# The row search of a routing front in four parts, step 0's sum a group sooner, lists joined in group 13, tokens taken earlier

## The reference, cut to what matters

```python
xn = layernorm(x)                                   # x: 2 x 4096 x 256, f32
# attention with 12 sampled positions per token and head (16 heads of 16)
off = tanh(pw_w @ gelu(depthwise_conv3(q)) + pw_b) * 6
positions = clip(token + anchor + off, 0, 4095)
scores = q . sample(k, positions) / 4 - rel_scale * |positions - token|
s = (softmax(scores) . sample(v, positions)) @ wo.T + bo
# mixture of experts: 8 experts, each token uses its best 2
g = silu(sum over 2 chosen experts of gate * (silu(a) * b) @ Wl2)
out = x + s * g
```

## Time and profile before

| | us |
|---|---|
| median of 3 runs (lowest, highest) | 1420.66 (1420.04, 1420.97) |
| the profiled execution | 1421.36 |
| its span, first to last instruction | 1419.6 |
| TensorE busy in the span | 1328.6 (94%) |
| VectorE busy | 1245.7 (88%) |
| ScalarE busy | 798.7 (56%) |
| GpSimd busy | 725.6 (51%) |
| mean granted TensorE clock | 0.968 |

### The profile page before, as it was taken

One profiled execution on the slowest core, in us unless ns is written; L12 is line 12 of the kernel. 1 busy time (PEld: TensorE's weight loads), 2 busy tenths in 40 slices (PEclk: granted clock), 3 DMA queues, 4 the chain that ended last, 5 costly groups with the idle time before them and its releaser, 6 DMA issues. The chain is left out here.

```text
span 1419.6 us, 36324 instructions
## 1 busy us (share of the span) xinstructions
PE 1328.6 (94%) x13885; PEld 1063.0 (75%) x13885; DVE 1245.7 (88%) x1759; ACT 798.7 (56%) x1920; POOL 725.6 (51%) x441
## 2 busy tenths in 40 slices
PE   4998899997899999999999999999999978998987
PEld 4864455655688888888888888888888866777775
DVE  7847788788699999999999999999999999898971
ACT  2546688866655454545554454555455446676654
POOL 1001022100477888787887888886887862211031
PEclk9999999996899999999999999999999989999997
DMA  7952556964758586868777585877777569989679
GB/s 242 345 184 88 149 183 201 297 203 141 222 169 270 136 256 169 246 192 242 203 221 216 148 262 139 234 192 236 201 199 214 142 168 277 293 222 266 196 214 208
DMA packets 206905, 297.77 MB, mean 210 GB/s; under 512 B 21809, under 2 KB 164533, under 8 KB 206515
## 3 DMA queue, kind: packets, MB, share of 16 engines
q0 software_dynamic: 59968, 141.95, 38.0%
q1 hardware_dynamic: 119171, 141.43, 31.1%
q10 hardware_dynamic: 27632, 12.64, 3.5%
HBM read 186.30 MB, written 118.03 MB: 214 GB/s over the span
## 5 line engine op out<-in xcount | busy, mean ns | idle before, releaser
L1651 POOL DMA_INDIRECT moe_rows<-expert_mem,token_of x135 | 333.2, 2468 | 105.5 <-issue 71.5
L1618 POOL DMA_INDIRECT expert_mem<-xn_rows,token_of x131 | 243.7, 1860 | 48.1 <-issue 38.1
L1941 PE MATMUL pY<-expert_mem 128*128 x1080 | 253.2, 386 | 0.0
L1941 PEld LDWEIGHTS pY<-expert_mem 128*128 128x128 f32 x1080 | 199.0, 190 | 39.4 <-issue 13.6
L2139 DVE SCALAR_TENSOR_TENSOR mid<-pos_pair,mid 128x768 f32<-128x768 f32 x224 | 197.3, 950 | 0.5
L1785 ACT ACTIVATE expert_mem<-pA,b1sel 128x256 f32<-128x256 f32 (+1 forms) x300 | 110.1, 455 | 126.3 <-PE pA L1935 120.5
L1935 PE MATMUL pA<-mid,expert_mem 128*128 128x256 f32 (+1 forms) x816 | 168.3, 360 | 5.5 <-ACT mid L1757 4.9
L262 DVE SCALAR_TENSOR_TENSOR mid<-mid 128x768 f32<-128x768 f32 x192 | 169.4, 949 | 0.0
L1935 PE MATMUL pB<-mid,expert_mem 128*128 128x256 f32 (+1 forms) x816 | 166.1, 357 | 0.0
L1796 ACT ACTIVATE expert_mem<-pB,b1sel 128x256 f32<-128x256 f32 (+1 forms) x300 | 110.7, 468 | 96.1 <-PE pB L1935 96.1
L1935 PEld LDWEIGHTS pA<-mid,expert_mem 128*128 128x128 f32 x816 | 143.4, 192 | 24.2 <-ACT mid L1757 3.9
(11 more groups left out here) (282 smaller groups left out, 2408.3 us busy)
## 6 DMA issues: line engine op xcount, KB each, us to landing
expert_mem<-in_w_l POOLq DMA_DIRECT2D x51, 1024.0 KB
bandT<-in_w_l POOLq DMA_DIRECT2D x24, 1024.0 KB
band<-band_rows SPq DMA_DIRECT2D x256, 96.0 KB, 5.4
S_rows<-expert_mem SPq DMA_DIRECT2D x64, 376.0 KB, 4.7
band_rows<-wgt SPq DMA_DIRECT2D x12, 1536.0 KB
pos_pair<-pos_rows SPq DMA_DIRECT2D x28, 384.0 KB
xn_rows<-expert_mem SPq DMA_DIRECT2D x16, 512.0 KB, 5.6
v_rows<-expert_mem SPq DMA_DIRECT2D x16, 512.0 KB, 4.5
```

What stands on the lines that cost most here:

```text
L1618: nc.gpsimd.indirect_dma_start(out=xs[:, u, s], out_offset=None, in_=dram["xn"], in_offset=bass.IndirectOffsetOnAxis(ap=keep["inv"][:, 2 * ...
L1651: nc.gpsimd.indirect_dma_start(out=dram["moe"], out_offset=bass.IndirectOffsetOnAxis(ap=keep["inv"][:, 2 * n + s:2 * n + s + 1], axis=0), ...
L1941: mm = nc.tensor.matmul(pY[:, s], hid[:, h, c, s * P:(s + 1) * P], w2[:, c, ds(e * D, D)], start=False, stop=(closes and c == HC - 1))
```

## The change

Four edits, all of order, none of what is computed. The row search `find_rows` is cut into `sum_counts`, `halves_of_experts`, `rows_of_runs` and `ranks_of_tokens`; in group 1 the two `offset_bias` calls stand between the first three, and the fourth goes to group 2. `OPENING_FROM` goes from 9 to 8 and `OPEN_AT` from 6 to 5, which moves `load_opening`, `load_second`, ScalarE's preparation of step 0 and the ten parts of its sum a group forward. `merge_lists` is cut in two, one before each `offset_bias`, and goes from group 12 to 13. `take_tokens` goes from behind `offset_bias(14, 1)` to right behind `convolve(15)`.

```diff
-PLACES_AT, EXPERTS_AT, MERGE_AT, TOKENS_AT = 7, 8, 12, 14
-OPEN_AT = 6
+PLACES_AT, EXPERTS_AT, MERGE_AT, TOKENS_AT = 7, 8, 13, 14
+OPEN_AT = 5
-OPENING_FROM = 9
+OPENING_FROM = 8
-            def find_rows():
+            def sum_counts():
                 dve.wait_ge(counts_taken, 1)
                 for e in range(EXPERTS):
                     ins = V.tensor_tensor_scan(upto[:, :, e], totals[:, :, e], ...)
                 chain(ins)
+            def halves_of_experts():
                 ...
+            def rows_of_runs():
                 chain(V.tensor_tensor(place, upto, totals, ALU.subtract))
                 ...
+            def ranks_of_tokens():
                 for k in range(TOPK):
                 ...
-            def merge_lists():
-                dve.wait_ge(pieces_loaded, 32)
-                for c, some in ((0, P), (1, LINEAR - P)):
-                    of = pieces[0:some, c]
-                    ...
-                dve.sem_inc(merged, 1)
+            def merge_lists(c, some):
+                if c == 0:
+                    dve.wait_ge(pieces_loaded, 32)
+                of = pieces[0:some, c]
+                ...
                 if n == COUNT_AT:
                     gate_values()
-                    find_rows()
-                if n > 0:
+                    sum_counts()
+                    offset_bias(n - 1, 0)
+                    halves_of_experts()
+                    offset_bias(n - 1, 1)
+                    rows_of_runs()
+                if n == COUNT_AT + 1:
+                    ranks_of_tokens()
+                if n > COUNT_AT:
                     if OPENING_FROM <= n < OPENING_FROM + 5:
                         open_step(n, 0)
                     ...
                     if n == MERGE_AT:
-                        merge_lists()
+                        merge_lists(0, P)
                     offset_bias(n - 1, 0)
-                if n > 0:
+                if n > COUNT_AT:
+                    if n == MERGE_AT:
+                        merge_lists(1, LINEAR - P)
+                        dve.sem_inc(merged, 1)
                     if OPENING_FROM <= n < OPENING_FROM + 5:
                         open_step(n, 1)
                     ...
             convolve(STEPS - 1)
+            take_tokens()
             positions(STEPS - 3)
             offset_bias(STEPS - 2, 0)
             offset_bias(STEPS - 2, 1)
-            take_tokens()
             offset_bias(STEPS - 1, 0)
```

More of the change, by code:

```diff
@@ L1226, in take_experts @@
                 V.tensor_copy(keep["tile_exp"][:], pOff[0:1, 1, 0:HIGH]).then_inc(experts_known, 1)
-            def merge_lists():
-                dve.wait_ge(pieces_loaded, 32)
-                for c, some in ((0, P), (1, LINEAR - P)):
-                    of = pieces[0:some, c]
[L1233 to L1238, removed]
-                dve.sem_inc(merged, 1)
+            def merge_lists(c, some):
+                if c == 0:
+                    dve.wait_ge(pieces_loaded, 32)
+                of = pieces[0:some, c]
+                chain(V.tensor_tensor(of[:, 0:CHAINS - 1], of[:, 0:CHAINS - 1], of[:, 1:CHAINS], ALU.subtract))
+                for q in range(CHAINS):
+                    ins = V.scalar_tensor_tensor(of[:, q], counting[0:some, 0:P], limit[0:some, c, q:q + 1], of[:, q], ALU.is_lt, ALU.mult)
+                chain(ins)
+                chain(V.tensor_tensor(of[:, 0:2], of[:, 0:2], of[:, 2:4], ALU.add))
+                chain(V.tensor_tensor(of[:, 0], of[:, 0], of[:, 1], ALU.add))
             def take_tokens():
```

## The result

The changed kernel takes 1410.22 us (median of 18 runs, 1401.82 to 1419.96); the kernel before took 1421.06 beside it (18 runs, 1410.33 to 1427.88). The ratio is 0.9937, with an interval of 0.9915 to 0.9959: faster by 6 to 12 us of 1421. The forecast was 1404.5 in a range of 1400 to 1413. The profiled execution took 1412.04, with a span of 1410.3 and a mean granted clock of 0.978 (0.968 before).

A forecast was written before the change was run, and what follows sets the result against it. The front was taken as bound by waits in a loop of TensorE, VectorE and ScalarE, the mix as full. Terms -5.3-8.2-2.7 = -16.2 take the median from 1420.66 to 1404.5 us; own range 1400 to 1408, with rivals 1400 to 1413.

The forecast's parts named there:

- The row search: Groups 1 to 4: biases between the search's parts end TensorE's 5.79 us wait; group 4's routing matmuls 5.3 us sooner.
- Step 0's sum and the lists: Groups 8 to 13: VectorE's extra work spread over groups; group 13's last bias sooner by 8.2 us, ends -9.2 and -5.
- a stop that goes: Group 11: the 2.12 us stop inside one set of head scores disappears, leaving the full -9.2 us.
- one that moves with the loads: Group 11's stop follows step 1's earlier loads and again lowers TensorE's level; 2.1 of the 9.2 us lost.
- The tokens: End of the front: gathers about 10 us sooner, last head scores whole; -2.7 us, ends -3.3 and +1.
- the shreds: Last head scores torn beside the gathers, 363.4 to 368.28 us for what takes 1.2; expected to go, worth 3.3 us.
- The sum: Whole kernel: the three terms together, -5.3-8.2-2.7 = -16.2 us, giving a median of 1404.5.
- The mix as long as before within 1 us: Expected sign after the front: the mix only begins and ends earlier; several us longer would show the forecast wrong.
- Rival 1: Front: shreds and stop belong to a place in TensorE's program, not to DMA; -12.4 us, 1408.3, chance 0.20.
- Rival 2: Groups 9 to 13: VectorE's longer rounds idle TensorE, which drops to its lower level; -7.7 us, 1413.0, chance 0.08.
- Rival 3: Start of the mix, held by loads or GpSimd, absorbs half the gain; -8 us, 1412.5, chance 0.05.
- Rivals 4 and 5: 4: loop stalls in groups 8 to 13, 1425.5, chance 0.04; 5: holes refill elsewhere, 1420.7, chance 0.03.

The follow-up runs named there:

- e5: The kernel before with only the row search in four parts: 1418.49 us, ratio 0.994.
- e12: Changed kernel, SyncE's second 1 MB weight load and GpSimd's first weight loads later, store cases appended: 1515.76 us whole, about 1404.6 estimated without the cases.
- e1: The kernel before, nothing edited, run and traced again: 1422.67 us, ratio 0.9987.
- e3: The kernel before with the scatters of expert results replaced by small plain stores, experts' sum left out: 1422.91 us, ratio 0.9991.
- e6: The kernel before with the row search split, step 0's sum a group sooner and lists joined in group 13, `take_tokens` not moved: 1410.98 us, ratio 0.9926.
- e7: The kernel before with only `take_tokens` moved to right behind `convolve(15)`: 1422.85 us, ratio 0.9984.
- e2: The changed kernel, nothing edited, run and traced again: 1408.49 us, ratio 0.9902 against the kernel before.
- e11: Nothing of the kernel: 24 indirect GpSimd stores beside eight kinds of work; idle stores took 0.96 to 1.12 us, beside one subtraction 5.16.

## Why the prediction was right, and where it was wrong

**The row search (-5.3).** Right, and a little short. The bias, `tanh(0)`, the projection and the routing matmuls came within 0.8 us of the walk; the new wait was 1.00, not 1.9, as the stop of 1.18 ahead of it made TensorE later. On the mean of five traces with the old front and four with the new the group 4 mark moved from 180.3 to 174.0: -6.3. Alone (e5) it moved to 173.8, and the median fell by 3.3. How much of it lasts to group 13 isn't settled by one trace (4.0 there).

**Step 0's sum and the lists (-8.2).** Right in the number, and partly by luck. Bias 13 was forecast at 325.4 and is at 323.2 to 323.7; the means moved from 337.7 to 323.4, which is -14.3 with the row search and -8.0 without. The choice inside this term, the middle between a stop that goes (-9.2) and one that moves with the loads (-7.1), has to be judged apart. The stop neither went nor moved with the loads of step 1: it stayed at its instruction and grew. From group 4 to bias 13 the old fronts took 157.3 on the mean, the changed ones 149.4, and e12, where the stop is gone, 146.0. So without a stop the term would be about -11.3 (an estimate from one trace), not -9.2, and the stop takes 3.4 of it back, not 1.1: two errors of over 2 us cancelled. Where the walk was 2 us short was not traced. The 5.25 and 6.43 of the earlier trace rows are gone as forecast.

**The tokens (-2.7).** Wrong, and this is the step that failed: "If the shreds belong to the gathers, they go". e1, e3, e5 and e6 run the gathers late and the last scores whole, and e7 gains nothing. The on which the term rested were one execution's chance; the front of another execution of the same program ended 8 us sooner.

**The sum (-16.2).** For the front it holds: 15.05 by timed runs of the fronts alone, 16.4 by the mean of the traces (366.9 to 350.5). In the place of the tokens' 2.7 stand 1.0 more from the row search and 2.1 won behind bias 13, and these 2.1 no term had: from there to bias 15 the old fronts take 29.2 us on the mean and the changed ones 27.1, but e6, without the tokens' move, takes 27.1 too, and e7, with it, 29.0. It goes with TensorE's level there (the windows under e12): it is the lower one for 10.2 us in the four traces that take 26.2 to 27.3, for 13.7 in three that take 27.6 to 28.1, and for 20.5 in five that take 28.6 to 29.1; the first trace, with its shreds, has 18.4 and 31.5. What sets that time was not tested, and that it fills the tokens' place is luck. For the whole kernel the sum doesn't hold: the medians fell by 10.8 and, in the second set, by 13.3. The first interval (6 to 12 us) shuts the forecast out, the second (9 to 19) does not. Both medians, 1410.22 and 1408.49, lie above the forecast's own range of 1400 to 1408, and inside 1400 to 1413 only as that takes in the rivals.

**"The mix as long as before within 1 us".** Wrong as an expectation of a trace: the stretch from 504 to 641 took 137.2 where it had taken 127.8. By the prediction's own last line this counts against it. It is no fixed effect of the change, since e7 has it and e2 doesn't; whether the tokens' move makes it likelier is open. The 2 to 4 us between the gain of the fronts alone and that of the whole kernels were not traced to a place; whole traces whose mix stretches differ by 9 us among themselves can't tell them.

**The rivals.** Rival 1 (stops by a place in the program) came closest in the number for the whole kernel: 12.4 against the 10.8 and 13.3 measured. On the front alone, where its terms lie, it is 2.7 short of 15.05 and the forecast 1.2 over, so that closeness is partly luck. It was right that the stop of `head_scores(11, 0)` keeps its place, which is the same instruction in twelve of thirteen traces, but e12 speaks against a stop that has nothing to do with DMA. It was right in its term of nothing for the tokens, though the shreds are not at such a place either. Rival 2 did not come: between groups 9 and 13 the lower level stands only behind the stop. Rival 3's number (8) is 2.8 from the first measurement, rival 1's 1.6; its mechanism, a start of the mix held by loads, isn't in the traces: where the mix lost time, it did so some 200 us later. Rivals 4 and 5 did not come.

## What to carry to other kernels

A loop over three engines, walked from the rows of one trace, was right within 1 us for where the engines meet in groups 2 to 4; over the ten groups behind them it was some 2 us off, which another error hid. The worth of moving VectorE's work out of such a loop could be read from it. What can't be read from one trace is a term made of stops at issue: trace the same program twice before a gain is booked on them. Cut the kernel at a stage's end and time the stage: the front alone told 15 us with a spread of 2 to 5, where the whole kernel told 11 to 13 with a spread of 13 to 21.

## What the runs showed of the hardware

**Stops at fixed places of TensorE's program.** Counting all of TensorE's instructions in the trace, those of its sequencer too, the sets of head scores from group 2 on are torn by over 0.7 us from one matmul to the next, with nothing but issue as the cause, at numbers 2240, 3264, 4544, 5056, 5824, 7616, 8128, 9920 and 10176, all 192 more than a multiple of 256, and nowhere else. The first trace of the kernel before has smaller tears of 0.58 to 0.70 at nine other places, six of them the shreds of the earlier trace rows; no other trace has them. At most of them most traces show nothing; number 7616 cost 1.5 to 3.7 us in twelve of thirteen traces and nothing in e12. Number 2240 cost 1.1 to 1.4 us in seven of the eight traces in which TensorE came to it at 146 to 148 with the DMA engines at 1.03 or more in the 2 us ahead, and nothing in the five in which it came at 152 to 154 with idle ones. The Trainium skill (Runtime: NRT & Kernel Launch, Instruction fetch mechanics) says that the code comes in blocks of 256 instructions, and that crossing one is "mostly hidden". The spacing agrees, and at most such places nothing shows; at 2240 and 7616, beside full DMA, the crossing was not hidden. That block fetches are the cause is an inference.

**One long VectorE instruction holds GpSimd's indirect store.** A store of 1.0 us took 5.16, and an adding one of 1.6 took 5.70 to 5.76, beside one 4.95 us subtraction with both operands in SBUF; eight products of 0.88 us in a row cost it 0.2. The Trainium skill (SBUF — State Buffer, SBUF: two separate sides) describes a port pair shared by VectorE and GpSimd as an exclusive lock, held for the whole instruction, also where VectorE has two SBUF inputs and GpSimd reads SBUF. The subtraction agrees, and so do the short products of e11 and e12, if GpSimd gets its turn between two of them; the five long stores beside such products in the mix don't fit. A kernel whose stores or gathers go through GpSimd may gain from cutting such instructions; that was not tried.
